# Mamba and mixture-of-experts tower on one core: decays in PSUM, scans in two halves, every second drive on POOL

## The reference

```
delta = softplus(dt_raw * W_dt[:, 0] + b_dt)
def step(h, inp):
    d_t, b_t, c_t, u_t = inp
    dA = exp(d_t[..., None] * A)
    h = dA * h + d_t[..., None] * b_t[:, None, :] * u_t[..., None]
    y = einsum('bds,bs->bd', h, c_t)
    return (h, y)
```

## Time and profile before

| | |
|---|---|
| median of 3 runs | 1308.86 us |
| the profiled execution | 1309.32 us, its span 1307.5 us |
| DVE busy | 1082.3 us, 83% of the span |
| PE busy | 1043.1 us, 80% |
| POOL busy | 664.6 us, 51% |
| ACT busy | 608.4 us, 47% |
| costliest group | scans L1209, 342.9 us in 176 instructions |
| the other two of the state loop | reads L1217, 183.5 us; drives L1201, 181.0 us in two groups |

### The profile page before, as it was taken

One profiled execution on the slowest core, in us unless ns is written; L12 is line 12 of the kernel. 1 busy time (PEld: TensorE's weight loads), 2 busy tenths in 40 slices (PEclk: granted clock), 3 DMA queues, 4 the chain that ended last, 5 costly groups with the idle time before them and its releaser, 6 DMA issues.

```text
span 1307.5 us, 16414 instructions
## 1 busy us (share of the span) xinstructions
PE 1043.1 (80%) x4783; PEld 793.6 (61%) x4783; DVE 1082.3 (83%) x1866; ACT 608.4 (47%) x1530; POOL 664.6 (51%) x801
## 2 busy tenths in 40 slices
PE   4778879788797887978879778676529999999980
PEld 4666657456574665756657556344318888888860
DVE  6689899899999999989989999999414467777773
ACT  1564444434545345453453544533006666666650
POOL 6000183561854818547075382773740067776675
PEclk7999889899898988988989989888759999999995
DMA  4598010020110201102011010014735679898882
GB/s 156 187 372 292 5 49 18 7 84 1 52 40 7 80 5 51 40 7 84 1 43 49 7 50 15 15 56 184 272 106 168 176 230 275 259 280 257 266 260 82
DMA packets 104361, 150.05 MB, mean 115 GB/s; under 512 B 13968, under 2 KB 91216, under 8 KB 103889
## 3 DMA queue, kind: packets, MB, share of 16 engines
q1 hardware_dynamic: 87377, 107.20, 25.2%
q0 software_dynamic: 16896, 41.80, 11.1%
HBM read 72.12 MB, written 76.82 MB: 114 GB/s over the span
## 4 chain that ended last, share of the span: by engine, by line
PE 38%; DVE 31%; issue 20%; POOL 4%; DMA 3%; SPq 1%; ACT 1%; DVEq 0%; POOLq 0%; ACTq 0%
PE BC L907 10%; DVE arena L1209 10%; PE Y L757 6%; DVE arena L1201 5%; PE K L919 5%; DVE arena L1217 5%; PE F L692 4%; PE Y L901 3%; PE K L769 2%; DMA mixer_own<-pool_dram 2%; PE F L705 2%; POOL pool_dram L602 2%; PE F L708 1%; PE F L913 1%; POOL gat L631 1%
## 5 line engine op out<-in xcount | busy, mean ns | idle before, releaser
L1209 DVE TENSOR_TENSOR_SCAN arena<-arena 128x888 f32<-128x888 f32 (+1 forms) x176 | 342.9, 1948 | 0.3
L757 PE MATMUL Y<-arena,ident 128*128 128x444 f32 (+1 forms) x704 | 328.0, 597 | 4.5 <-DVE arena L1217 4.5
L602 POOL DMA_INDIRECT pool_dram<-hrow,slot_of x176 | 241.3, 1371 | 60.6 <-issue 52.7
L631 POOL DMA_INDIRECT gat<-y_dram,slot_all x176 | 176.6, 1003 | 144.8 <-DMA y_dram<-mixer_own 87.9
L983 ACT ACTIVATE arena<-mixer_own,aneg 128x216 f32<-128x216 f32 (+1 forms) x384 | 145.5, 453 | 188.5 <-DVE arena L1209 142.4
L983 ACT ACTIVATE arena<-arena,aneg 128x216 f32<-128x216 f32 x320 | 124.7, 464 | 169.0 <-DVE arena L1209 128.6
L739 PE MATMUL BC<-bc_rows,sel 96*128 96x222 bf16 (+1 forms) x352 | 66.5, 273 | 157.8 <-DVE arena L1217 157.7
L757 PEld LDWEIGHTS Y<-arena,ident 128*128 128x128 f32 x704 | 135.3, 212 | 83.9 <-issue 74.5
L907 PE MATMUL BC<-arena,xt 128*128 x716 | 185.4, 382 | 0.0
L1217 DVE TENSOR_TENSOR arena<-arena,BC 128x888 f32<-128x888 f32 (+1 forms) x176 | 183.5, 1042 | 0.0
L535 POOL TENSOR_TENSOR seen<-seen,count 128x32 f32<-128x32 f32 x10 | 16.5, 1649 | 270.6 <-ACT count L1027 270.6
(11 more groups left out here) (214 smaller groups left out, 1603.7 us busy)
## 6 DMA issues: line engine op xcount, KB each, us to landing
mixer_own<-pool_dram SPq DMA_DIRECT2D x179, 144.0 KB, 3.7
y_dram<-mixer_own SPq DMA_DIRECT2D x179, 128.0 KB
pool_dram<-filler SPq DMA_DIRECT2D x5, 4176.0 KB, 29.5
arena<-in_experts_dram SPq DMA_DIRECT2D x1, 7680.0 KB, 21.3
arena<-in_x_dram SPq DMA_DIRECT2D x10, 648.0 KB, 4.2
pool_dram<-filler SPq DMA_DIRECT2D x1, 4896.0 KB, 32.2
arena<-in_experts_dram SPq DMA_DIRECT2D x1, 4608.0 KB
pool_dram<-hrow,slot_of POOLq DMA_INDIRECT x176, 2.8
```

Of the source, the lines that this page charges most:

```text
L602: nc.gpsimd.indirect_dma_start(out=pool_rows, out_offset=bass.IndirectOffsetOnAxis(ap=slot_of[q][0:r, b, k:k + 1], axis=0), in_=hrow[q][0: ...
L631: nc.gpsimd.indirect_dma_start(out=gat[0:r, k, b, :], out_offset=None, in_=y_rows[0:blocks_by(t) * P, :], in_offset=bass.IndirectOffsetOnA ...
L757: mm = nc.tensor.matmul(Y[j][:, 0:w], ident[:], read[g % 3][:, j * w:(j + 1) * w], start=False, stop=(s == STATES - 1), skip_group_check=True)
L1209: nc.vector.tensor_tensor_scan(state[g % 2][:, 0:w], decay[g % 3][:, 0:w], drive[g % 2][:, 0:w], 0.0, ALU.mult, ALU.add).then_inc(scan_don ...
```

## The change

- Decays are written by ACT into two PSUM banks, `D[0]` for channel groups 0 and 1 and `D[1]` for groups 2 and 3; there is no second copy. `decays(g, b)` waits for the half scan of state g - 1 on the same bank.
- A scan is two scans of 444 elements (`scan(g, 0)`, `scan(g, 1)`), with a semaphore count for each.
- For odd s the drive is multiplied on POOL (`drives` there) from a copy of B in SBUF that ACT makes (`copy_b`), four buffers deep; for even s it stays on DVE. `spread(g)` now puts C of state g and B of state g + 1 in its bank.
- The four banks F0, F1, K0, K1 become two, F and K: the convolution's two halves follow each other in F, the projection to B and C moves to K, and many pieces move to other slots.
- POOL's scatter of a tile is spread over slots 1 to 10 of the next tile but one, its allocation over slots 12 to 15, and the drives stand between them.

The core of the diff:

```diff
-        decay = [carve(KI * N) for _ in range(3)]
         at_drive = taken[0]
-        drive = [carve(KI * N) for _ in range(2)]
+        drive = [carve(KI * N) for _ in range(DRIVES)]
         state = [carve(KI * N) for _ in range(2)]
         read = [carve(KI * N) for _ in range(3)]
-        assert taken[0] == ARENA
+        b_row = [carve(N) for _ in range(B_ROWS)]
...
-        F = [ps("F0"), ps("F1")]
-        K = [ps("K0"), ps("K1")]
-        PX, PG, PH, PY = Y, BC, F, K
+        D = [ps("D0"), ps("D1")]
+        F = ps("F")
+        K = ps("K")
...
+        def by_pool(g):
+            return g % STATES % 2 == 1
+
+        def pooled(g):
+
+            return sum(by_pool(n) for n in range(g))
+
...
+            def drives(g):
+
+                i = g // STATES
+                pool.wait_ge(b_copied, pooled(g + 1))
+                if g % STATES == 1:
+                    pool.wait_ge(du_done, i + 1)
+                if g >= DRIVES:
+                    pool.wait_ge(scan_done, 2 * (g - DRIVES + 1))
+                nc.gpsimd.tensor_tensor(cut(drive[g % DRIVES], i), cut(du[i % 2], i),
+                                        b_row[pooled(g) % B_ROWS][:, None, 0:width(i)].broadcast_to([P, KI, width(i)]), ALU.mult
+                                        ).then_inc(drive_done, 1)
...
+            def pieces(i, s):
+                t, n = i - 1, i + 1
+                back, mix, front = i >= 1, 0 <= i < TILES, n < TILES
+                if i >= 2 and mix and 1 <= s <= 10:
+                    for at in range(8 * (s - 1) // 5, 8 * s // 5):
+                        scatter(i - 2, at // TOPK, at % TOPK)
+                if back and s == 5:
+                    refine_mixed(t)
+                if back and mix and s in (12, 13, 14):
+                    if s == 12:
+                        allocating[0] = allocation(t)
+                    next(allocating[0])
+                if front and s == 13:
+                    multiply_series(n)
+                if back and mix and s == 15:
+                    close(t)
                     if i == TILES - 1:
...
+            allocating = [None]
+            for i in range(-1, TILES):
+                for s in range(STATES):
+                    g = STATES * i + s
+                    if 0 <= g + 2 < STATES * TILES and by_pool(g + 2):
+                        drives(g + 2)
+                    pieces(i, s)
+            for at in range(2 * TOPK):
+                if at == TOPK:
+                    refine_mixed(TILES - 1)
+                scatter(TILES - 2, at // TOPK, at % TOPK)
+            for at in range(2 * TOPK):
+                scatter(TILES - 1, at // TOPK, at % TOPK)
...
+                if c == 2 and k == 0:
+                    pe.wait_ge(x2_done, 2 * n + 1)
                 w = width(n)
-                to = F[c // 2][:, (c % 2) * w:(c % 2 + 1) * w]
+                to = F[:, (c % 2) * w:(c % 2 + 1) * w]
...
+            def project_bc(n):
+                if n > 1:
+                    pe.wait_ge(base_done, n - 1)
...
+                if (g + 1) % STATES == 0 and g + 1 < STATES * TILES:
+                    pe.wait_ge(bc_split, SPLITS * ((g + 1) // STATES + 1))
+                    if g < 0:
                         pe.wait_ge(sel_step, 4)
+                if g == 1:
+                    pe.wait_ge(own_drive, 1)
                 if g >= 2:
                     pe.wait_ge(read_done, g - 1)
-                w = width(i)
-                for j in range(2):
-                    mm = nc.tensor.matmul(BC[g % 2][:, j * w:(j + 1) * w], sel[:, STATES * j + s, :], bc_rows[i % 2][:, 0:w],
-                                          start=True, stop=True)
+                for j, state_ in ((0, g + 1), (1, g)):
+                    if 0 <= state_ < STATES * TILES:
+                        i, s = divmod(state_, STATES)
+                        w = width(i)
+                        mm = nc.tensor.matmul(BC[g % 2][:, j * N:j * N + w], sel[:, STATES * j + s, :], bc_rows[i % 2][:, 0:w],
+                                              start=True, stop=True)
                 mm.then_inc(bc_done, 1)
...
+            def copy_b(g):
+
+                w = width(g // STATES)
+                act.wait_ge(bc_done, g + 1)
+                if pooled(g) >= B_ROWS:
+                    act.wait_ge(drive_done, pooled(g) - B_ROWS + 1)
+                nc.scalar.activation(b_row[pooled(g) % B_ROWS][:, 0:w], BC[(g - 1) % 2][:, 0:w], ACT.Copy).then_inc(b_copied, 1)
...
+            def decays(g, b):
                 i, s = divmod(g, STATES)
-                if g >= 3:
-                    act.wait_ge(scan_done, g - 2)
-                elif g == 0:
+                if g >= 1:
+                    act.wait_ge(scan_done, 2 * (g - 1) + b + 1)
+                elif b == 0:
                     act.wait_ge(mixer_setup, 1)
-                if s == 0:
+                if s == 0 and b == 0:
                     act.wait_ge(delta_done, i + 1)
                 w = width(i)
-                for c in range(KI):
+                for c in range(2):
                     last = nc.scalar.activation(
-                        decay[g % 3][:, c * w:(c + 1) * w].rearrange("p (a t) -> p a t", t=TOKENS)[:, :, 1:TOKENS],
-                        cut(delta[i % 2], i)[:, c, :].rearrange("p (a t) -> p a t", t=TOKENS)[:, :, 1:TOKENS],
-                        ACT.Exp, scale=aneg[:, s, c:c + 1])
+                        D[b][:, c * w:(c + 1) * w].rearrange("p (a t) -> p a t", t=TOKENS)[:, :, 1:TOKENS],
+                        cut(delta[i % 2], i)[:, 2 * b + c, :].rearrange("p (a t) -> p a t", t=TOKENS)[:, :, 1:TOKENS],
+                        ACT.Exp, scale=aneg[:, s, 2 * b + c:2 * b + c + 1])
                 last.then_inc(decay_done, 1)
...
+                if front and s == 3:
+                    tanh_conv(n, 0)
+                if back and s == 6:
+                    normalise(t)
+                    copy_h1t(t)
+                if back and s == 7:
+                    logit_exp(t)
+                if front and s == 8:
+                    tanh_conv(n, 1)
+                if back and s == 9:
+                    shared_gate(t)
+                if front and s in (10, 11):
+                    take_dt(n, 2 * (s - 10))
+                    take_dt(n, 2 * (s - 10) + 1)
+                if back and mix and s == 11:
+                    take_ranks(t)
+                if front and s == 11:
+                    softplus_exp(n)
                 if s == 13:
+                    if mix:
+                        tanh_gate(i, 0)
                     if front:
                         softplus_series(n)
-                    if mix:
-                        tanh_gate(i, 1)
-                    if front:
                         nc.scalar.preload_act_table_set("natural_log_exp_and_others")
                         softplus_ln(n)
+                if mix and s == 15:
+                    tanh_gate(i, 1)
...
             def split(n):
                 w, at = width(n), SPLITS * n
-                rows, bank = bc_rows[n % 2], F[1]
+                rows, bank = bc_rows[n % 2], K[:, N:2 * N]
                 dve.wait_ge(rows_done, n + 1)
+                if n > 1:
+                    dve.wait_ge(rank_taken, n - 1)
...
             def drives(g):
+                i = g // STATES
+                dve.wait_ge(bc_done, g + 1)
+                if g % STATES == 0:
+                    dve.wait_ge(du_done, i + 1)
+                nc.vector.tensor_tensor(cut(drive[g % DRIVES], i), cut(du[i % 2], i),
+                                        BC[(g - 1) % 2][:, None, 0:width(i)].broadcast_to([P, KI, width(i)]), ALU.mult
+                                        ).then_inc(own_drive, 1)
+
+            def scan(g, b):
                 i, s = divmod(g, STATES)
-                dve.wait_ge(bc_done, g + 1)
-                if s == 0:
-                    dve.wait_ge(du_done, i + 1)
-                nc.vector.tensor_tensor(cut(drive[g % 2], i), cut(du[i % 2], i),
-                                        BC[g % 2][:, None, 0:width(i)].broadcast_to([P, KI, width(i)]), ALU.mult).then_inc(drive_done, 1)
-
-            def scan(g):
-                i = g // STATES
-                w = KI * width(i)
-                dve.wait_ge(decay_done, g + 1)
-                dve.wait_ge(drive_done, g + 1)
-                nc.vector.tensor_tensor_scan(state[g % 2][:, 0:w], decay[g % 3][:, 0:w], drive[g % 2][:, 0:w], 0.0, ALU.mult,
+                lo, hi = 2 * b * width(i), 2 * (b + 1) * width(i)
+                dve.wait_ge(decay_done, 2 * g + b + 1)
+                if b == 0:
+                    if by_pool(g):
+                        dve.wait_ge(drive_done, pooled(g + 1))
+                    else:
+                        dve.wait_ge(own_drive, g + 1 - pooled(g + 1))
+                nc.vector.tensor_tensor_scan(state[g % 2][:, lo:hi], D[b][:, 0:hi - lo], drive[g % DRIVES][:, lo:hi], 0.0, ALU.mult,
                                              ALU.add).then_inc(scan_done, 1)
 
```

(12 more changed lines are left out.)

327 lines of the change are left out of this document (149 added, 178 removed).

## The result

The changed kernel takes 1324.78 us in the median of 19 runs, the kernel before 1309.27 us in 19 runs beside them. The medians lie 1.2% apart; the ratio of the means is 1.0079, 95% interval 1.0050 to 1.0108. The change makes the kernel **slower, by 0.8% in the mean**, where 1296 us was forecast.

A forecast was written before the change was run, and what follows sets the result against it. DVE's own work was taken to bound the first phase. Savings of 91.5 us, less waits of 15.3, 26, 13 and 19.9 and ends of 4.8, gave -12.5: 1296 us, range 1258 to 1322.

The forecast's parts named there:

- Work off DVE: First phase: 88 drives move from DVE to POOL, -82.8 us; a second half scan 176 times, +15.8 us.
- Waits for B and C: DVE's drives behind slot 10's two projections: waits for PE all gone once these stand apart, -24.5 us.
- Wait A: Scan of state 8 waits for ACT's decays, behind POOL's drive, scatters and layer norm: 1.7 us in 9 tiles, +15.3.
- Wait B: Second SiLU in slot 8 waits for ACT's tanh behind PE's chain: 3.0 us in 8 tiles, +26 us.
- Wait C: Split in slot 11 waits for ACT to take the ranks from bank K: 1.3 us in ten tiles, 13 us.
- Wait D: Softplus in slot 14 waits for POOL's series product behind a drive and small operations: 2.1 us in 9 tiles, +19.9.
- Ends: Prologue: convolution halves share F, +1.5 us; end: last scatter and `refine_mixed` come later, +3.3 us.
- the second eight: POOL's second eight scatters at the end cost nothing, as POOL had 4.4 us to spare before the last scatters.
- the first: Rival, chance 0.22: waits A to D are mostly hidden; at half the time is 1259 us, with none 1222.
- The second: Rival, chance 0.14: POOL's drives are held for scans, so waits A and D each grow 2 us in 9 tiles: 1332.
- The third: Rival, chance 0.06: PSUM costs each of 352 half scans 0.05 us or more, cancelling the gain; 1319 at 0.065.
- The fourth: Rival, chance 0.13: gain and waits cancel, and the time is within 4 us of before.

The follow-up runs named there:

- experiment 8: Kernel before, with ten matmuls of zeros behind the shared expert's last one in slot 9 of tiles 1 to 9: 1313.7 us.
- experiments 1 to 3: Changed kernel, each alone: POOL's norm root ahead of the drive, 1283.8 us; POOL's series product ahead of allocation, 1295.7; ACT's ranks ahead of delta's last takes, 1297.7.
- experiment 6: Changed kernel with TensorE matmuls of zeros in idle stretches of slots 9 and 15: 1307.7 us; in slot 9 alone 1304.9, in slot 15 alone 1315.1.
- experiment 7: Changed kernel with zero matmuls on TensorE in slot 9 and in slot 6 ahead of the normed rows' turn, tiles 1 to 9: 1298.5 us.
- experiment 5: Changed kernel with each half scan reading its drive from SBUF for both inputs in place of decays from PSUM: 1394.5 us.

## Why the prediction was wrong

It failed by waits that it put at nothing; the four waits that it walked through came true. In us, forecast and measured:

- Work off DVE, -82.8 + 15.8 = -67.0: its busy time fell from 1082.3 to 1014.8, -67.5. The sum is right by luck, since both terms are too large and the errors cancel. DVE's timeline in the changed kernel, an odd slot and an even one:

```profile
459.45 2.03 DVE L1283 TENSOR_TENSOR_SCAN arena<-D,arena 128x444 f32<-128x444 f32 x2
461.40 1.05 DVE L1270 TENSOR_TENSOR arena<-arena,BC 128x888 f32<-128x888 f32 x1
462.38 1.07 DVE L1295 TENSOR_TENSOR arena<-arena,BC 128x888 f32<-128x888 f32 x1
463.36 2.04 DVE L1283 TENSOR_TENSOR_SCAN arena<-D,arena 128x444 f32<-128x444 f32 x2
465.44 1.08 DVE L1295 TENSOR_TENSOR arena<-arena,BC 128x888 f32<-128x888 f32 x1
```

A pair of half scans with a drive behind it takes 1.95 us start to start, where the whole scan took 1.92: the second half costs about 0.03 us, not 0.09. And with the drive gone the read starts 2.08 us behind the scans, so that a drive less saves 0.85 us and not 0.97. By this the terms are some +5 and -73 us. DVE's operations held by POOL also weigh in: `slot_of`, 16 elements from one SBUF input, takes 1.05 us in nine tiles in place of 0.17 with all drives on DVE, 8 us in all.

- Waits for B and C, -24.5: gone. They were not the order of the projections alone, as the prediction had it; about 8 us of them were TensorE's half clock (experiment 8).
- Wait A, +15.3: 14.7. Wait B, +26: 26.6. Wait C, +13: 10.4. Wait D, +19.9: 21.0. All four at the place and in the chain that the walk gave; experiments 1 to 3 took A, D and C away by their causes, and B down to 7.9. Together 74.2 forecast, 72.7 measured.
- Ends, +1.5 and +3.3: the first scan starts 1.9 later (50.32 against 48.38), and from the last gate to the first of the last scatters it takes 30.8 us in place of 24.9, +5.8: the 8 scatters ahead of the last root could start only at 938.78, 4.8 us behind the last gate, since most of the last allocation now stands behind the last drive in POOL's queue. Undersized by 3 us. That POOL had time to spare for the second eight came true: it stands idle for 4.54 us ahead of the last scatters.
- **Not in the sum:** the residual's wait, 14.8, and the moments' of all tiles but the last, 8.3 (12.4 less 4.1). With some 3 us of idle time before the reads (2.8 in the row by form above) that is 26 of the 28 us missed.

The step that failed is the one on TensorE. I added its half clock in wait B alone ("after such idling its add-up took 3.20 instead of 1.67; I add 1.2 us") and dismissed PE elsewhere by its busy time ("PE's 67.4 us stay below a tile's 81"). A busy time under the tile's length does not say that each result is there when DVE reads it. The residual shows it. PE around slot 9 in the kernel before:

```profile
477.47 1.03 PE L807 MATMUL K<-sharedw,hid_s 128*111 128x256 f32 x4
483.95 0.55 PE L739 MATMUL BC<-bc_rows,sel 96*128 96x222 bf16 x2 [5.45 <-DVE arena L1217]
```

The idle stretch of the routing and the sums of 3.20 us behind it were there before the change. But the shared expert's last matmul ran ahead of them, 11 us before the residual read it (488.75), and the residual waited nowhere. The change moved the shared expert behind the router, and this matmul into the slot of the residual: it now stands behind the idle stretch and the slow sums, and is read as soon as it ends. Order and clock make this wait together: with zeros in the idle stretch it is gone (experiment 6). For the moments, PE idles 7.70 us in slots 14 and 15, of which wait D is 2.3, and works at the half clock behind that; zeros there take their wait from 12.4 to 5.7 us, 4.1 of it the last tile's (11.8 without zeros there, experiment 7). Experiment 7 gives the size in time: without the half clock behind two of the idle stretches the changed kernel takes 1298.5 us. That the zeros of slot 15 don't shorten the kernel further goes with the growth of wait B (experiment 6); a kernel with zeros in all three stretches was not run.

Of the rivals: the first (waits half hidden) is refuted, they came in full. The second (POOL's drives held by scans) is refuted, 1.91 us; with decays in SBUF too (experiment 5), the scans are held and not the drives. The third (a fixed cost of PSUM in half scans) is refuted, 1.06 us. The 65 ns that the Trainium skill, "VectorE: DVE Perf Modes", TRN2 errata, would add to each half scan don't appear. The fourth, that gain and waits cancel, had 0.13 and describes the lower value, not the median. The range, up to 1322, ended 3 us short.

## What to carry to other kernels

When work is taken off the busiest engine, walk through each other engine's queue and ask what stands ahead of the work that the busiest one will now wait for sooner: here a few lines moved up turned a loss of 0.8% into a gain of 4.4%. Then do the same for TensorE: list its idle stretches, take what stands behind each at the half clock, and ask how soon it is read; a busy time below the tile's length does not answer that. And compare kernels at the same granted clock.
